# Second attention of a two-layer gated block on the context's own 64 columns, with tiles paired on halves of TensorE's array

## The chip, the cores and the metric

One core of one Trainium2 chip. The metric is the time of the whole kernel on the device in microseconds; lower is better. All operands are float32 unless a tile is declared BF16. The matrix engine is TensorE (PE), the others are VectorE (DVE), ScalarE (ACT), GpSimd (POOL) and SyncE (SP), which issues most DMAs.

## The reference

x has 4 batches of 256 rows of 128 (1,024 rows, 8 tiles of 128 rows); the context ctx_512 has 4 batches of 512 rows of 64. LN is a layer norm without weights.

```python
x = x + tanh(g_xattn[0]) * attention16(LN(x), ctx_512)       # self and cross attention, 16 heads of 8
x = x + tanh(g_ffn[0])   * routed_experts(LN(x))             # 8 experts, top 2, capacity 160 each pass
# second attention: one head of 128, over the context alone
q = LN(x) @ Wq + bq                  # Wq 128x128
k = ctx_512 @ Wk + bk                # Wk 64x128
v = ctx_512 @ Wv + bv                # Wv 64x128
x = x + tanh(g_xattn[1]) * softmax(q @ k.T) @ v
# dense experts: all 8 are computed for every row, 2 of them get a weight
x = x + tanh(g_ffn[1]) * sum_e c_e * (silu(h @ w1g_e.T) * (h @ w1u_e.T)) @ w2_e.T,  h = LN(x)
```

## The kernel before, in words

**The first layer** (lines 830 to 1461) is the attention with 16 heads and the routed experts. Here it matters in three places. At the start GpSimd makes constants (lines 679 to 726), the last two being the ones of the value tiles, and then helps to split queries and keys (`qk_r`, line 743). Then TensorE turns the 24 blocks of expert weights (`turn_weights`, line 1819) while ScalarE copies them out of PSUM (`take_weights`), and GpSimd puts the rows at their experts' slots (line 797); SyncE reads them back as `xs` (lines 644 and 646). `routed_experts` starts with `transpose_rows(0)`, which waits for those rows.

**Between the weights and the routed experts** stands `context(j)` on TensorE (line 1994): four products of 65x512 give the second attention's keys for the whole context (`k1_t`), sixteen of 65x128 give its values (`v1`). Row 64 of `c_t`, the turned context, holds ones for the bias. ScalarE copies the results out (lines 1039 to 1046). The first expert's products wait for these copies (`kv1_act`).

**The second attention** (TensorE from line 2064, ScalarE from 1081, VectorE from 1490) takes the rows that the routed experts have written back, in three groups, `BACK = ((0, 2), (2, 4), (4, 8))` tiles. `turn_back` turns the normalised rows, `queries1` multiplies them by Wq. Then per tile t, with two tiles (`QT`) to a batch: `scores1` (one product, 128x512), VectorE's `max1`, ScalarE's `exp1`, four turnings of the probabilities on TensorE (line 2091), ScalarE's `take_turned1`, `values1` (four products of 128x128), VectorE's `add_values` and row statistics. The order written out is: scores of t + 1, turning of t, values of t - 1. `unread(n)` are bf16 products of 512 columns that nobody reads.

**The dense experts** (`dense_experts`, lines 1935, 1375 and 1019) need the normalised rows of four tiles (`normalise(3, s)`), turned (`transpose_half(3, s)`) and copied (`take_ht`). Per unit i, that is a half s and an expert e: a pair of products of 128x512 on TensorE (line 1957), Silu on ScalarE, a product with `hidden` on VectorE (line 1399), four products down (line 1945), and `take_down` on VectorE. Units 0 to 14 follow each other in order; behind the pair of unit 1 `go_down(0)`, `transpose_half(3, 1)`, the pair of unit 2 and the router.

Semaphores that count: `p_in`/`p1_in` probabilities, `q1_act` queries copied, `x3_in` rows of the second attention finished, `hh_in` hidden products.

## Time and profile before

| | |
|---|---|
| median of 3 runs | 333.73 us (333.17 to 334.24) |
| profiled execution, span | 337.6 us; the page gives no other time of its own |
| TensorE busy | 312.9 us, 93% |
| VectorE busy | 220.8 us, 65% |
| ScalarE busy | 194.1 us, 57% |
| GpSimd busy | 115.7 us, 34% |
| mean granted clock of TensorE | 0.995 of full speed |

The span is from the first to the last instruction of one profiled execution, from which all starts and durations below come. A line number of a row is that of the kernel file. A float32 product appears as two matmul records, a float32 turning (transpose) as one. Records of products overlap in time since they are pipelined; in the chain of waits each piece has only the time that it adds.

### The profile page before, as it was taken

Reading aid. Unit: us, or ns where it says so; the run is one execution under the profiler, and the core shown is the slowest. Engines: PE = TensorE matmul, PEld = TensorE weight load, DVE = VectorE, ACT = ScalarE, POOL = GpSimd, SP = SyncE. Lnnn points to the kernel's source line nnn. Section 1 sums busy time; section 2 is a strip of 40 time slices with the busy share of each in tenths; the row PEclk is TensorE's granted clock in tenths of the full one; section 3 lists DMA queues with packets and bytes.
Section 4 is the critical chain, followed back from the end, with each engine's and each line's share of the span. In section 5 each row is a group of like instructions: output and inputs, shape, how many; then the busy total and the mean of one; then the engine's idle time right before and its main releaser. Section 6 shows DMA issues by size and latency. Waiting matters only on the chain.

```text
span 337.6 us, 7474 instructions
## 1 busy us (share of the span) xinstructions
PE 312.9 (93%) x2891; PEld 189.6 (56%) x2891; DVE 220.8 (65%) x532; ACT 194.1 (57%) x410; POOL 115.7 (34%) x200
## 2 busy tenths in 40 slices
PE   8998969989999999899977999999996899999995
PEld 3545733334443434344666677777794357776665
DVE  4998798888989889676242052333321956779665
ACT  3468588978888889787266733323336265512221
POOL 6476732327334333231775003444442211110000
PEclk9999999999999999999997999999999999999999
DMA  7855995940437006240441580000002200000101
GB/s 174 199 110 160 175 213 132 209 90 10 153 110 209 5 5 188 70 124 2 109 157 35 133 212 10 21 18 19 22 12 70 71 0 2 1 2 0 31 3 31
DMA packets 35827, 27.83 MB, mean 82 GB/s; under 512 B 5627, under 2 KB 33070, under 8 KB 35792
## 3 DMA queue, kind: packets, MB, share of 16 engines
q1 hardware_dynamic: 33965, 25.04, 29.7%
q0 software_dynamic: 1280, 1.88, 1.7%
q10 hardware_dynamic: 547, 0.44, 0.5%
q8 instruction: 23, 0.38, 0.5%
q14 instruction: 12, 0.10, 0.1%
HBM read 11.89 MB, written 5.26 MB: 51 GB/s over the span
## 4 chain that ended last, share of the span: by engine, by line
PE 73%; ACT 7%; DVE 6%; issue 5%; POOL 5%; DMA 2%; SPq 0%; DVEq 0%; POOLq 0%; ACTq 0%
PE psum L1682 11%; PE psum L1876 11%; PE psum L1957 8%; PE psum L1624 5%; PE psum L1648 5%; PE psum L1945 4%; PE psum L1864 4%; ACT qk_r L948 3%; PE psum L1814 2%; POOL rows_in L797 2%; PE psum L1651 2%; PE psum L2060 2%; PE psum L2052 1%; PE psum L1575 1%; PE psum L1869 1%
## 5 line engine op out<-in xcount | busy, mean ns | idle before, releaser
L1213 DVE TENSOR_REDUCE nmax<-psum 128x2 f32<-128x1024 f32 (+2 forms) x88 | 102.0, 1216 | 11.6 <-PE psum L1624 10.3
L948 ACT ACTIVATE parts<-psum 128x512 f32<-128x512 f32 (+1 forms) x88 | 45.2, 566 | 8.6 <-PE psum L1648 7.7
L1876 PE MATMUL psum<-p_more,kcat 128*128 128x320 f32 (+2 forms) x160 | 40.2, 396 | 0.9 <-DVE p_more L1346 0.7
L819 POOL DMA_INDIRECT rows_back<-qcat,back_at x24 | 22.9, 952 | 50.3 <-ACT qcat L981 43.1
L1876 PEld LDWEIGHTS psum<-p_more,kcat 128*128 128x128 f32 x160 | 26.1, 190 | 9.1 <-issue 0.9
L1350 DVE TENSOR_TENSOR qcat<-psum,qk_r 128x320 f32<-128x320 f32 (+2 forms) x40 | 16.6, 422 | 22.1 <-ACT qk_r L989 13.5
L989 ACT ACTIVATE qk_r<-psum 128x320 f32<-128x320 f32 (+2 forms) x40 | 15.2, 384 | 24.5 <-PE psum L1876 21.5
L1682 PE MATMUL psum<-parts,v_aug 128*18 128x256 f32 (+1 forms) x352 | 28.5, 369 | 0.0
L1957 PE MATMUL psum<-h_t,kcat 128*128 128x512 f32 x60 | 28.1, 594 | 0.0
L1682 PE MATMUL psum<-qk_r,v_aug 128*18 128x256 f32 (+1 forms) x160 | 27.4, 373 | 0.0
L1648 PE MATMUL psum<-qcat,kcat 64*128 64x256 bf16 x256 | 24.7, 271 | 1.9 <-ACT p_more L948 0.8
L1027 ACT ACTIVATE qk_r<-psum 128x512 f32<-128x512 f32 x15 | 9.0, 597 | 30.1 <-PE psum L1957 30.1
L1682 PE MATMUL psum<-qk,v_aug 128*18 128x256 f32 (+1 forms) x160 | 26.1, 363 | 0.0
L1624 PE MATMUL psum<-kcat,qcat 64*128 64x512 bf16 x128 | 24.9, 386 | 0.2 <-DMA qcat<-parts 0.2
L1346 DVE COPY p_more<-psum 128x320 f32<-128x320 f32 x8 | 3.9, 492 | 29.7 <-PE psum L1854 29.7
L948 ACT ACTIVATE qk_r<-psum 128x512 f32<-128x512 f32 (+1 forms) x40 | 21.0, 581 | 2.1 <-PE psum L1648 1.7
L948 ACT ACTIVATE qk<-psum 128x512 f32<-128x512 f32 (+1 forms) x40 | 20.0, 551 | 1.8 <-PE psum L1648 1.8
L971 ACT ACTIVATE kcat<-psum 128x512 f32<-128x512 f32 x24 | 12.9, 607 | 13.0 <-PE psum L1814 7.8
L1945 PEld LDWEIGHTS psum<-kcat,qcat 128*128 128x128 f32 x120 | 15.6, 191 | 6.3 <-issue 5.0
L1624 PEld LDWEIGHTS psum<-kcat,qcat 64*128 64x128 bf16 x128 | 6.1, 93 | 22.6 <-issue 11.9
L797 POOL DMA_INDIRECT rows_in<-h_rows,put_at x16 | 16.0, 1000 | 8.1 <-issue 5.2
L690 POOL TENSOR_SCALAR ln_rstd<-ln_mv 128x2 f32<-128x2 f32 (+2 forms) x10 | 2.6, 261 | 41.7 <-DVE ln_mv L1118 22.8
(249 smaller groups left out, 630.4 us busy)
## 6 DMA issues: line engine op xcount, KB each, us to landing
kcat<-parts SPq DMA_DIRECT2D x18, 192.0 KB, 3.8
qcat<-parts SPq DMA_DIRECT2D x21, 128.0 KB, 3.6
kcat<-ones_b SPq DMA_DIRECT2D x8, 192.0 KB, 4.6
kcat<-in_L_ffn_wi_gate_dram SPq DMA_DIRECT2D x6, 256.0 KB, 4.5
kcat<-in_L_ffn_wi_up_dram SPq DMA_DIRECT2D x6, 256.0 KB, 4.8
kcat<-in_L_ffn_wo_dram SPq DMA_DIRECT2D x6, 256.0 KB, 5.0
parts<-in_L_ffn_w_dram SPq DMA_DIRECT2D x3, 512.0 KB, 5.6
rows_in<-zeros SPq DMA_DIRECT2D x1, 1290.0 KB, 5.7
```

The lines of the kernel that those rows point to most:

```text
L797: pool.indirect_dma_start(out=rows_in[0:E * SLOTS, :], out_offset=bass.IndirectOffsetOnAxis(ap=put_at[:, k, t:t + 1], axis=0), in_=h_rows[ ...
L819: pool.indirect_dma_start(out=rows_back[:, :], out_offset=bass.IndirectOffsetOnAxis(ap=back_at[0:m, e, t:t + 1], axis=0), in_=eo[0:m, e % ...
L948: act.activation(p_slots[u % NPT][:, 0:w], s2_bank(s2_place[u])[:, 0:w], ACT.Exp, scale=SCALE).then_inc(p_in, 1)
L989: act.activation(sg[:, i % 2, 0:m], gate_up_bank(i, 0)[:, 0:m], ACT.Silu).then_inc(sg_in[0], 1)
L1213: dve.tensor_reduce(dst[:, :, n * g:n * (g + 1)], src.rearrange("p (r q k) -> p r q k", r=PAR, q=n), AX.X, ALU.max, negate=True).then_inc( ...
L1350: dve.tensor_tensor(hh[:, e % 2, f, first:end], gate_up_bank(i, 1)[:, 0:end - first], sg[:, i % 2, 0:end - first], ALU.mult).then_inc(hh_i ...
L1624: ins = pe.matmul(dst, q[:, S + t * P:S + (t + 1) * P], k[:, S:KW], start=True, stop=True)
L1648: ins = pe.matmul(dst[:, c * S:(c + 1) * S], k[:, key:key + P], q[:, S:QW], start=True, stop=True)
L1682: ins = pe.matmul(dst[:, cols], v_aug[:, at:at + 2 * HA], p, start=r == 0 and opens(n), stop=r == ROUNDS - 1, skip_group_check=True)
L1876: ins = pe.matmul(gate_up_bank(i, m)[:, 0:end - first], w_t[e][:, m, f * P:(f + 1) * P], xs_t[:, e % 2, first:end], start=True, stop=True)
L1945: ins = pe.matmul(bank(DN_BANK[n % 4])[:, t * P:(t + 1) * P], hh1[:, n % 2, t * P:(t + 1) * P], w1_t[:, e, 2, :], start=True, stop=True)
L1957: ins = pe.matmul(bank(2 + 2 * (i % 2) + m), w1_t[:, e, m, :], h_t[:, s * BANK:(s + 1) * BANK], start=True, stop=True)
```

## The change

The second attention no longer makes keys and values. With M = Wq Wk^T (128x64), the scores of a row h are (h M + bq Wk^T) times the context's own row, plus a number per row, h (Wq bk) + bq bk. So:

- `fold_weights1` on TensorE, in the place of `context`: turns `w1_q` and `w1_k`, and multiplies them into `mk` (M, the bias column, the offset column), with 3 unread products inside and 16 behind it. ScalarE makes `bq_wide` and two copies.
- `queries1` multiplies by M (64 columns out); a batch's two tiles go to PSUM rows 0 to 63 and 64 to 127. `offsets1` makes the number per row. `scores1(b)` does both tiles of a batch, each on 64 rows of the array, against `c_t`, whose rows 64 to 127 are now a second copy of the context.
- `max1` has a second instruction, which takes the offset off the maximum by a subtraction and adds it again (`s1_bias`).
- `sums1(b)` multiplies the turned probabilities by the context's rows (64 columns out, two tiles on the halves of the columns), VectorE copies the sums (`take_sums1`), and `values1(b)` multiplies both tiles at once by Wv, laid out twice in the block diagonal `w1_v2`. The value bias times the gate is added to x beforehand (`add_value_bias`).
- The order on all three engines is written out tile by tile. The first dense pair, `gate_up1(0)`, stands between `sums1(3)` and `values1(3)`; the wait for `x3_in` goes from unit 1 to unit 2.
- SyncE loads the context's rows again (`ctx_rows`) and copies `c_t` to its other half behind the dense experts' weights. GpSimd clears `w1_v2` at the start, and multiplies `b1v` by the gate ahead of the masks.
- Dense halves are turned into banks 2 and 1, not 0 and 1.

The diff, cut to its core:

```diff
+            sp.dma_start(ctx_rows, c_in).then_inc(ctx_again, 16)
+            sp.dma_start(c_t[DC:2 * DC, :], c_t[0:DC, :]).then_inc(ctx_again, 16)
...
+            pool.memset(w1_v2[:, :], 0.0).then_inc(w1v_zero, 1)
...
+                link(pool.tensor_scalar(b1v[:, :], b1v[:, :], tanh_g[:, 1:2], None, ALU.mult))
...
+            act.wait_ge(gw_in, 1)
+            act.activation(bq_wide, zeros[:, 0:D], ACT.Identity, bias=b1_col[:, :]).then_inc(bq_in, 1)
+            act.wait_ge(mk_full, 1)
+            act.activation(w1_turned, bank(TURN1_BANK)[:, 0:D + DC + 1], ACT.Copy).then_inc(mk_act, 1)
+            act.wait_ge(mk_full, 2)
+            act.activation(mk, bank(MK_BANK)[:, 0:MK_OFF + 1], ACT.Copy).then_inc(mk_act, 1)
...
+            take_offsets(0)
+            take_queries(1)
+            take_offsets(1)
             exp1(0)
-            take_queries(1)
-            for t in range(NT):
-                if t + 1 < NT:
-                    exp1(t + 1)
+            exp1(1)
+            take_turned1(0)
+            take_rows(2)
+            take_turned1(1)
+            exp1(2)
+            take_queries(2)
+            exp1(3)
+            take_offsets(2)
+            take_turned1(2)
+            take_turned1(3)
+            for t in range(4, NT):
+                exp1(t)
+            for t in range(4, NT):
                 take_turned1(t)
...
+                link(dve.tensor_reduce(s1_nmax[:, t:t + 1], s1_bank(t), AX.X, ALU.max, negate=True))
+                if t in (0, BACK[1][0], BACK[2][0]):
+                    dve.wait_ge(off1_in, [first for first, _ in BACK].index(t) + 1)
+                dve.scalar_tensor_tensor(out=s1_bias[:, t:t + 1], in0=s1_nmax[:, t:t + 1], scalar=s1_off[:, t:t + 1],
+                                         in1=s1_off[:, t:t + 1], op0=ALU.subtract, op1=ALU.add).then_inc(nm1_in, 1)
...
+            statistics(2, 2, x_sb)
             max1(0)
-            statistics(2, 2, x_sb)
-            for t in range(NT):
-                if t + 1 < NT:
-                    max1(t + 1)
-                reciprocal1(t)
-                if t == 0:
-                    normalise(2, 2, x_sb)
-                if t >= 1:
-                    add_values(t - 1)
-                if t == NT - 2:
-                    normalise(3, 0, x1_sb)
-            add_values(NT - 1)
+            max1(1)
+            normalise(2, 2, x_sb)
+            max1(2)
+            max1(3)
+            add_value_bias(0, TPH)
+            reciprocal1(0)
+            max1(4)
+            take_sums1(0)
+            max1(5)
+            add_values(0)
+            reciprocal1(1)
+            take_sums1(1)
+            max1(6)
+            max1(7)
+            add_values(1)
+            add_value_bias(TPH, NT)
+            reciprocal1(2)
+            take_sums1(2)
+            normalise(3, 0, x1_sb)
+            add_values(2)
+            reciprocal1(3)
+            take_sums1(3)
+            add_values(3)
...
+            def fold_weights1():
+
+                dst = bank(TURN1_BANK)
+                pe.transpose(dst[:, 0:D], w1_q[:, :], ident[:, :])
+                pe.transpose(dst[:, D:D + DC + 1], w1_k[:, :], ident[0:DC + 1, 0:DC + 1]).then_inc(mk_full, 1)
+                unread(N_UNREAD_FOLD)
+                pe.wait_ge(mk_act, 1)
+                pe.wait_ge(bq_in, 1)
+                pe.wait_ge(wt_in[0], W_LAST[MK_BANK] + 1)
+                wq, wk, dst = w1_turned[:, 0:D], w1_turned[:, D:D + DC + 1], bank(MK_BANK)
+                pe.matmul(dst[:, 0:DC + 1], wq, wk, start=True, stop=True)
+                for t in range(QT):
+                    pe.matmul(dst[t * DC:(t + 1) * DC, MK_BIAS:MK_BIAS + 1], wk[:, 0:DC], b1_col[:, :], start=True, stop=True)
+                pe.matmul(dst[:, MK_OFF:MK_OFF + 1], bq_wide, wk[:, DC:DC + 1], start=True, stop=True).then_inc(mk_full, 1)
+
+            fold_weights1()
+            unread(N_UNREAD_ROWS)
...
+                for t in range(first, end):
+                    dst = bank(Q1_BANK)[t % QT * DC:(t % QT + 1) * DC, (t - first) // QT * P:((t - first) // QT + 1) * P]
+                    ins = pe.matmul(dst, mk[:, 0:DC], h_t[:, t * P:(t + 1) * P], start=True, stop=True)
+                ins.then_inc(q1_full, 1)
...
+            def scores1(b):
+                pe.wait_ge(q1_act, next(s + 1 for s, (first, end) in enumerate(BACK) if QT * b < end))
+                if b == 0:
+                    pe.wait_ge(ctx_again, 32)
+                    pe.wait_ge(wt_in[1], E)
+                if b >= 2:
+                    pe.wait_ge(p1_in, QT * (b - 1))
+                for t in range(QT * b, QT * b + QT):
+                    half = slice(t % QT * DC, (t % QT + 1) * DC)
+                    pe.matmul(s1_bank(t), q1_t[half, b, :], c_t[half, b * SC:(b + 1) * SC],
+                              start=True, stop=True).then_inc(sc1_full, 1)
+
+            def turn1(t):
                 b = t // QT
-                pe.matmul(bank(t % 2), q1_of(t, t + 1), k1_t[:, b * SC:(b + 1) * SC],
-                          start=True, stop=True).then_inc(sc1_full, 1)
-
-            def values1(t):
-                pe.wait_ge(p1t_in, t + 1)
-                if t >= 2:
-                    pe.wait_ge(x3_in, t - 1)
+                pe.wait_ge(p1_in, t + 1)
+                if b >= 1:
+                    pe.wait_ge(p1t_in, t - QT + 1)
+                else:
+                    pe.wait_ge(off1_in, 2)
                 for c in range(CT):
-                    ins = pe.matmul(bank(4 + t % 2)[:, 0:D], p1_t[:, t % 2, c * P:(c + 1) * P], v1[:, CT * (t // QT) + c, :],
-                                    start=(c == 0), stop=(c == CT - 1))
-                ins.then_inc(o1_full, 1)
+                    ins = pe.transpose(bank(t % QT)[:, c * P:(c + 1) * P], p1[:, b % 2, t % QT, c * P:(c + 1) * P],
+                                       ident[:, :])
+                ins.then_inc(p1t_full, 1)
+
+            def sums1(b):
+                pe.wait_ge(p1t_in, QT * b + QT)
+                if b == 0:
+                    pe.wait_ge(q1_act, len(BACK))
+                else:
+                    pe.wait_ge(u1_in, b)
+                for c in range(CT):
+                    for t in range(QT):
+                        ins = pe.matmul(bank(U1_BANK)[t * DC:(t + 1) * DC, 0:P], ctx_rows[:, CT * b + c, :],
+                                        p1_t[:, b % 2, t, c * P:(c + 1) * P], start=(c == 0), stop=(c == CT - 1),
+                                        skip_group_check=True)
+                ins.then_inc(u1_full, 1)
+
+            def values1(b):
+                pe.wait_ge(u1_in, b + 1)
+                if b == 0:
+                    pe.wait_ge(off1_in, len(BACK))
+                else:
+                    pe.wait_ge(x3_in, QT * b)
+                pe.matmul(bank(O1_BANK)[:, 0:QT * D], u1_t[:, b % 2, :], w1_v2[:, :], start=True, stop=True).then_inc(o1_full, 1)
...
-            unread(2)
+            unread(1)
             scores1(0)
             turn_back(1)
+            offsets1(0)
+            unread(1)
+            queries1(1)
+            unread(2)
             scores1(1)
-            queries1(1)
-            for t in range(NT):
-                if 0 < t < NT - 1:
-                    scores1(t + 1)
-                pe.wait_ge(p1_in, t + 1)
-                if t >= 2:
-                    pe.wait_ge(p1t_in, t - 1)
-                elif t == 0:
-                    pe.wait_ge(wt_in[1], E)
-                for c in range(CT):
-                    ins = pe.transpose(bank(2 + t % 2)[:, c * P:(c + 1) * P], p1[:, t % 2, c * P:(c + 1) * P], ident[:, :])
-                ins.then_inc(p1t_full, 1)
-                if t == QUERIES_AT:
-                    queries1(2)
-                if t >= 1:
-                    values1(t - 1)
-                if t == ROWS_AT:
-                    turn_back(2)
+            offsets1(1)
+            unread(1)
+            turn1(0)
+            turn1(1)
+            turn_back(2)
+            queries1(2)
+            offsets1(2)
+            turn1(2)
+            scores1(2)
+            turn1(3)
+            sums1(0)
+            scores1(3)
+            values1(0)
+            sums1(1)
+            turn1(4)
+            values1(1)
+            turn1(5)
+            turn1(6)
+            sums1(2)
+            turn1(7)
+            values1(2)
             transpose_half(3, 0)
-            values1(NT - 1)
+            sums1(3)
+            gate_up1(0)
+            values1(3)
             dense_experts()
```

## Rows read from the trace of the kernel before

**Rows 1.** windows: us, busy us of each engine (instructions), PEclk, DMA share, GB/s

```profile
184.50:191.50 7.00, 7.00 (x42) 5.08 (x41) 0.00 (x0) 5.00 (x9) 0.00 (x0) 1.00 0.41 107
265.00:275.70 10.70, 9.60 (x44) 5.33 (x44) 8.68 (x34) 5.44 (x13) 2.38 (x4) 1.00 0.00 0
275.70:289.90 14.20, 13.93 (x91) 10.96 (x92) 8.74 (x37) 8.31 (x19) 1.27 (x2) 1.00 0.01 2
```

**Rows 2.** chain of waits, start-up and before the routed experts: start, us added, what

```profile
21.64 1.65 POOL qk_r L743
...
180.05 4.50 PE psum L1814 x24
184.55 3.44 PE psum L2002 x8
187.99 3.57 PE psum L2006 x32
```

**Rows 3.** chain of waits, second attention and first dense units

```profile
265.26 0.50 PE psum L2036 x2
265.75 0.43 PE psum L2028 x2
...
280.11 0.86 PE psum L2052 x2
280.97 0.44 PE psum L2091 x4
281.41 0.89 PE psum L2060 x8
...
289.92 3.49 PE psum L1957 x8
...
294.74 1.72 PE psum L1957 x4
296.46 1.68 PE psum L1842 x16
```

**Rows 4.** timeline of ScalarE, two places: start, duration, instruction

```profile
185.23 0.60 ACT L971 ACTIVATE kcat<-psum 128x512 f32<-128x512 f32 x1 [0.39 <-PE psum L1814]
...
269.45 0.69 ACT L1072 ACTIVATE qk<-psum,s_nmax 128x512 f32<-128x512 f32 x1 [0.20 <-DVE s_nmax L1466]
```

**Rows 5.** groups by line from 190 us: busy us, mean ns | idle before

```profile
L1399 DVE TENSOR_TENSOR qcat<-psum,qk_r 128x512 f32<-128x512 f32 x15 | 10.4, 690 | 9.5 <-ACT qk_r L1027 9.5
...
L1027 ACT ACTIVATE qk_r<-psum 128x512 f32<-128x512 f32 x15 | 9.0, 597 | 30.1 <-PE psum L1957 30.1
...
L1466 DVE TENSOR_REDUCE s_nmax<-psum 128x1 f32<-128x512 f32 x8 | 5.5, 682 | 2.3 <-PE psum L2052 2.3
...
L1478 DVE SCALAR_TENSOR_TENSOR x_sb<-psum,s_rec,x_sb 128x128 f32<-128x128 f32 x8 | 2.8, 351 | 4.2 <-PE psum L2060 3.7 <-DVE s_rec L1488 0.4
...
L1470 DVE BATCH_NORM_STATS2 ln_stats<-x_sb 128x6 f32<-128x128 f32 x8 | 2.1, 282 | 0.0
...
L1488 DVE TENSOR_TENSOR s_rec<-s_rec,tanh_g 128x1 f32<-128x1 f32 x8 | 1.3, 160 | 0.3
```

**Rows 6.** line 646, the second load of each expert's rows, SyncE

```profile
L646 SPq DMA_DIRECT2D parts<-rows_in x8: 451/451/525, 186.0 to 194.0; - x8
...
DMA to landing us min/median/max: 2.0/2.3/2.3
```

**Rows 7.** timeline of GpSimd at start-up

```profile
21.00 0.55 POOL L726 MEMSET v_aug<- 128x256 f32 x1
```

**Rows 8.** timeline of TensorE in pass 1, bf16 scores on row halves

```profile
102.28 0.39 PE L1624 MATMUL psum<-kcat,qcat 64*128 64x512 bf16 x2
```

**Rows 9.** chain of waits, routed experts' products on column halves

```profile
201.83 0.61 PE psum L1869 x16
```

**Rows 10.** windows around the low granted clock, columns as in rows 1

```profile
179.00:180.00 1.00, 0.00 (x0) 0.00 (x0) 0.20 (x2) 0.69 (x2) 0.49 (x1) 1.00 0.18 58
...
181.00:182.00 1.00, 1.00 (x7) 0.97 (x6) 0.69 (x3) 1.00 (x3) 0.76 (x1) 0.50 0.14 43
```

199 lines of the change are left out of this document (106 added, 93 removed).

## The prediction

> **What bounds the kernel now.** I read the windows by stretch first, then the chain of waits, then the groups by line. The windows [rows 1] show TensorE busy for all of 184.5 to 191.5, for 9.6 of 10.7 us up to 275.7 and for 13.93 of 14.20 us up to 289.9, while VectorE has 8.74 and ScalarE 8.31 us of work in the last stretch: TensorE sets the pace there, the others have room. The chain [rows 2] gives the first stretch to the context projections, 3.44 + 3.57 = 7.0 us. It gives the second attention a period of 0.86 (scores) + 0.44 (turning) + 0.89 (values) = 2.19 us per tile [rows 3], then the dense products, which run without a gap from 289.92 to the end. So the end moves by whatever moves (a) the first routed expert and (b) the point from which dense products are gapless, the third pair at 294.74 [rows 3].
>
> **Part 1, the projections become a folded weight.** Removed: 7.0 us of TensorE. Added: two turnings (0.2), three unread products (0.215 each by the pair that takes 0.43 [rows 3]: 0.65), a wait for ScalarE, four small products, sixteen unread products (3.45). ScalarE ends its last weight copy near 185.8 [rows 4], then widens the bias and copies 193 columns, together at most what 512 columns cost, 0.59 [rows 5], which lets TensorE go on near 186.5. The four small products are bound by weight loads; the router's eight products with 8 columns take 1.68, 0.21 each [rows 3], two of ours have half the columns: 0.7. Then 187.2 + 3.45 = 190.7, against 191.5 where the projections end (184.55 + 7.0). Rows cannot be turned much earlier anyway: the first two loads issue by 186.0 and land 2.3 us later, near 188.5 [rows 6]. Gain 0.7; I take **-0.6**, bounds -1.2 (all small products hidden) and 0. The expert loop behind is TensorE's own work and keeps the gain. Two new transfers of 0.5 MB each are queued on SyncE behind the expert weights; behind them there only stands the read back, which waits for the last expert anyway: 0.
>
> **Part 2, start-up.** GpSimd clears w1_v2 (128x256) ahead of the value ones; the same size takes 0.55 [rows 7], and the chain runs through GpSimd right behind it, at 21.64 [rows 2]. Bounds 0 and +0.55; the chain behind is largely TensorE, so I take **+0.4**. The product for b1v on GpSimd stands ahead of masks, and TensorE's values wait for masks; today's block of three there delays nobody, so 0, its own length if that cover is gone. One more small load on SyncE, and its wait for the clearing some 30 us old: 0.
>
> **Part 3, the second attention.** TensorE's work from the first turned row to the third dense pair, before: turned rows 16 x 0.11, unread 4 x 0.215, queries 1.72 (1,024 columns, two times the 0.86 of 512), scores 8 x 0.86, turning 8 x 0.44, values 8 x 0.89, two dense pairs 3.44 (3.49 in the chain), one down product group, four of 128 columns like the values, 0.89: 26.2 us, from 265.26 to 294.74 [rows 3], so 3.3 idle. After:
> - Scores of two tiles on row halves. The bf16 scores of pass 1 do this: two of 512 columns take 0.39 together, so they start together [rows 8]. So a pair 0.91, 4 x 0.91 = 3.64, for 6.88; bound 1.72 a pair if the halves don't run together.
> - Queries on column halves, 8 products of 128 columns. The routed down products on halves take 0.61 for 8 of 64 columns [rows 9]; one after another 8 x 0.111 = 0.89, fully paired 0.44. I take 0.17 each (0.11 to 0.22): 1.4.
> - Sums: 32 products of 128 columns on column halves; serial 1.78 a batch, paired 0.89. I take 1.0 a batch. Values: 4 of 256 columns, 0.43 each.
> - Offsets, 8 with one column, weight-bound: 0.21 each, 1.7. Three more unread: 0.65.
>
> New work: 23.5 us, 2.7 less. That gain needs VectorE and ScalarE to keep pace, and this is where I expect it to fail. VectorE's work per tile: maximum 0.69, value add 0.35, row statistics 0.28, two small ones 0.16 [rows 5], 1.64. New are per tile a bias instruction that waits for the maximum (0.17 and a gap of 0.04), per batch a copy of the sums (128 columns; between 0.16 for one and 0.69 for 512 that is 0.29), and twice an addition over 512 columns (0.69 [rows 5]), less four pairs of small instructions: 8 x 0.21 + 4 x 0.29 + 1.4 - 4 x 0.39 = +2.7. And each wait in VectorE's order holds what is behind it.
>
> I laid the four queues out, each instruction at the later of its engine being free and its semaphore, with durations as above, 0.75 for an exponential and its read of the sum (the first alone 0.69 [rows 4]) and 0.59 for ScalarE's copies of 512 columns. For the kernel before this gives 290.05 for the first dense pair and 294.82 for the third (trace: 289.92 and 294.74 [rows 3]). For the new one:
> - statistics of the last four tiles stand ahead of the first maximum, and the first exponential also waits for offsets 1: it starts at 271.9, not 269.45 [rows 4].
> - queries 2 need rows 2 and tiles 0, 1 turned: the third batch's scores start at 277.3; VectorE sits idle 3.2 us before maximum 4.
> - maximum 5 stands behind the sums copy, maxima 6 and 7 behind add_values(0), reciprocals and sums copy 1: exponentials 6 and 7 end at 285.7. ScalarE turns tile 4 only behind them, though it was ready at 282.6. TensorE idles 2.3 us before turning tile 6.
> - sums 2 end near 288, normalise(3,0) stands behind their copy; first dense pair 290.8. It holds values(3) for 1.72: VectorE idles 1.8, and hidden(0) starts at 294.8, statistics, GpSimd and normalise(3,1) behind it: third pair **297.5**.
>
> So idle grows from 3.3 to 8.7, +5.4 for -2.7 of work: +2.7 against the layout of the kernel before. Bounds: +1.7 with queries, sums, gaps at their low ends, +5.6 with the column halves serial. From the third pair on the queues are as before. The early product itself is worth nothing here: what follows waits for VectorE.
>
> A rule against the sum: today the change from whole-array products to column halves and back shows 0.61 where full pairing is 0.44, so entry and exit cost at most 0.09 each [rows 9]. The new order has 21 such changes. I put them in TensorE's idle time, 0; all on the path they are 1.9, and the sum below would be +4.4. The Trainium skill (TensorEngine Tiling (Array Packing), Key Properties) says that a change of tiling mode drains TensorE; the trace agrees only as far as those 0.09 us leave room for a short drain.
>
> **Sum.** -0.6 + 0.4 + 2.7 = +2.5. The profiled span is 337.6, the median of the three runs 333.73; the page gives no other time of that execution. I add the difference to the median: **336.2 us**. A measurement can tell about 0.3% (1.0 us) from no change.
>
> **Rivals.**
> 1. *TensorE still sets the pace.* VectorE and ScalarE run ahead enough for idle time to stay at 3.3; then the 2.7 us of work come off: -2.7 - 0.6 + 0.4 = -2.9, **330.8**. For it: 14.20 us hold 8.74 of VectorE [rows 1]. Against: the waits in its queue. It decides if maxima 4 to 7 follow each other without waits, that is if tile 4 is turned before 284. Chance 0.17; a halfway case within 1.0 of no change 0.10.
> 2. *The clock falls.* TensorE was idle about 2 us from 178.1 and the granted clock went from 1.00 to 0.50 (2.4 to 1.2 GHz) from 181 [rows 10]; 24 turnings took 4.50 [rows 2] for 24 x 0.11 = 2.64. My layout has idle times of 2.3 us at 284 and about 1 us near 186. A fall costs 4.50 - 2.64, about 1.9: **338.1**. Chance 0.15.
> 3. *Row halves run one after another in f32*, so scores don't do what the change says: +3.2 more, **339.4**. Chance 0.05; no f32 product on row halves is in the trace, bf16 ones are.
> 4. *The tiling changes cost 0.09 each on the path*: 336.2 + 1.9 = **338.1**, chance 0.04. The drain that the Trainium skill (same page and section) names would be this case.
> The rest, 0.49, is the forecast, 334.7 to 337.8.
>
> **Numbers.** The likeliest case is 336.2. Slower by over 0.3%: 0.49 + 0.15 + 0.05 + 0.04 = 0.73; within 0.10; faster 0.17. The range goes from 332.0, leaving out most of rival 1, to 338.8, leaving out rival 3 and the high bound of the halves.
>
> **What would show it.** The first routed turning 0.6 earlier; the experts' cadence unchanged; the first exponential 2.5 us later relative to the first turned row; two scores in 0.9 together; VectorE idle some 3 us before maximum 4, TensorE some 2 us before turning tile 6; the third dense pair 2.7 us later against the first turned row; granted clock 1.00 throughout. I am wrong if TensorE's idle time there stays under 5 us, if the sums take 1.8 a batch, or if the early part shifts by over 1 us.

## The result, and the profile after

| | before | after |
|---|---|---|
| median | 333.57 us (333.17 to 334.24, 4 runs) | 336.62 us (336.10 to 339.91, 4 runs) |
| ratio after to before | | 1.0104, 95% interval 1.0066 to 1.0142 |
| profiled execution, span | 337.6 us | 334.7 us, its own time 336.49 us |
| mean granted clock | 0.995 | 0.999 |

The change costs 1.04%, 3.05 us; the forecast was 336.2. A time is its span plus 1.7 to 1.8 us in every execution that gives both, so the profiled execution of before, with its span of 337.6, must have taken about 339.4 us, well over its median; adding a difference to the median, as the forecast did, allows for that. The spans of the two profiles must not be subtracted. The kernel before was therefore profiled again with the first experiments (`before_again`: span 333.5, time 335.32). Executions with a mean granted clock of 0.998 or more are called undisturbed below; in the profiled ones of the others the clock stood at or near 0.50 for 2 us or more, and the others are mostly 1 to 3 us longer.

**The second attention.** The chain of waits of the kernel after, from the first turned row to the third dense pair, answers to [rows 3]:

```profile
259.32 0.49 PE psum L2103 x2
259.82 0.43 PE psum L2066 x2
...
264.18 1.06 PE psum L2134 x4
265.24 0.55 PE psum L2121 x4
266.08 0.68 ACT qk L1104 x2
266.80 0.66 PE psum L2145 x4
...
269.91 0.98 PE psum L2121 x8
270.89 0.50 PE psum L2145 x4
271.39 1.06 PE psum L2134 x4
...
277.44 0.61 DVE s_nmax L1507
...
279.96 0.50 ACT qcat L1112
...
280.59 0.63 PE psum L2145 x4
281.22 1.02 PE psum L2157 x16
...
285.09 1.91 PE psum L2006 x4
287.00 0.45 PE psum L2168 x2
287.44 0.02 issue
287.47 0.61 DVE x_sb L1532 x2
...
289.28 1.04 POOL ln_rstd L714
...
290.75 1.10 PE psum L1902 x4
291.84 1.72 PE psum L2006 x4
```

L2103 turns the rows, L2134 makes the scores of a pair of tiles, L2121 the offsets, L2145 turns the probabilities, L2157 makes the sums, L2168 the values, L2006 is a dense pair. The stretch takes 291.84 - 259.32 = 32.52 us. Before it took 29.48 [rows 3], and 29.49 in `before_again` (261.15 to 290.64). That is +3.04. In all three profiles the end comes 42.86 us after the third pair (334.7 - 291.84, 337.6 - 294.74, 333.5 - 290.64). The medians differ by 3.05 us. So, as near as the medians can tell, the whole difference lies in this stretch, and the change ahead of it is worth about nothing.

Windows over just this stretch, with the columns of [rows 1], first `before_again`:

```profile
261.15:290.64 29.49, 28.38 (x155) 19.15 (x156) 20.66 (x81) 16.23 (x35) 4.72 (x7) 1.00 0.00 1
```

then the kernel after:

```profile
259.32:291.84 32.52, 28.31 (x192) 17.00 (x193) 23.10 (x87) 16.41 (x38) 5.06 (x7) 1.00 0.00 1
```

TensorE is busy as long as before, 28.3 us, though its products should need 2.7 us less; VectorE has 2.4 us more; TensorE's idle time grows from 1.1 to 4.2 us. The timelines of VectorE and of ScalarE show where it waits:

```profile
272.54 0.69 DVE L1507 TENSOR_REDUCE s_nmax<-psum 128x1 f32<-128x512 f32 x1 [3.57 <-PE psum L2134]
...
265.81 0.26 ACT L1096 ACTIVATE s_off<-psum,qcat 128x2 f32<-128x2 f32 x1 [1.76 <-PE psum L2121]
265.98 0.68 ACT L1104 ACTIVATE qk<-psum,s_bias 128x512 f32<-128x512 f32 x1
...
278.33 0.69 ACT L1104 ACTIVATE qk<-psum,s_bias 128x512 f32<-128x512 f32 x1 [2.27 <-DVE s_bias L1510]
```

VectorE stands 3.57 us before maximum 4. ScalarE stands 2.27 us before exponential 6, because maxima 6 and 7 are in VectorE's line behind the values of batch 0 (277.44 in the chain). TensorE in turn stands 1.96 us before it turns tile 6, at 280.59. This is one chain: a wait in one engine's fixed order is passed on to the next.

**Ahead of the experts.** The chain of the kernel after no longer runs through products there; it answers to [rows 2]:

```profile
180.36 0.97 POOL rows_in L822
181.33 0.30 issue
181.63 2.22 DMA rows_in<-h_rows,put_at
...
184.26 2.21 DMA parts<-rows_in
186.51 0.66 PE psum L1920 x3
...
187.90 3.47 PE psum L1942 x12
```

GpSimd sends the rows to the experts in 16 puts from 161.08 on. The last put's own transfer takes 2.22 us, a load brings the rows back in 2.21 us, and TensorE, done with the sixteen unread products, waits 0.53 us for them (L1920 is the first routed turning).

### The profile page after: what moved, and what is told of

Read it like the earlier page. It is cut to its first block, busy times and chain, and to the rows that moved or that the text cites. A ratio compares the mean times of both kernels' runs of the same rounds, so it can differ in the third digit from the quotient of the medians.

```text
span 334.7 us, 7533 instructions
## 1 busy us (share of the span) xinstructions
PE 309.5 (92%) x2917; PEld 183.5 (55%) x2917; DVE 223.7 (67%) x538; ACT 190.3 (57%) x408; POOL 116.7 (35%) x202
## 4 chain that ended last, share of the span: by engine, by line
PE 68%; ACT 8%; POOL 7%; DVE 6%; DMA 5%; issue 5%; SPq 1%; DVEq 0%; ACTq 0%; POOLq 0%
PE psum L1748 11%; PE psum L1942 11%; PE psum L2006 7%; PE psum L1690 5%; PE psum L1714 5%; POOL rows_in L822 4%; PE psum L2020 4%; PE psum L1930 4%; ACT qk_r L973 3%; PE psum L1717 2%; PE psum L1641 1%; PE psum L2134 1%; PE psum L1935 1%; ACT parts L973 1%; DMA x_sb<-in_x_dram 1%
## 5 line engine op out<-in xcount | busy, mean ns | idle before, releaser
L2006 PE MATMUL psum<-h_t,kcat 128*128 128x512 f32 x60 | 28.3, 594 | 0.0
L713 POOL TENSOR_SCALAR ln_rstd<-ln_mv 128x2 f32<-128x2 f32 (+2 forms) x10 | 2.7, 273 | 44.2 <-DVE ln_mv L1523 22.3
```

Of the source, the lines that this page charges most:

```text
L2006: ins = pe.matmul(bank(2 + 2 * (i % 2) + m), w1_t[:, e, m, :], h_t[:, s * BANK:(s + 1) * BANK], start=True, stop=True)
```

## The experiments

The median of the undisturbed executions of the kernel before, taken anew beside each of three groups of experiments, is 333.6, 333.5 and 333.8 us (13 of 25, 14 of 22 and 5 of 13 executions); for the kernel after it is 336.5 (three of four). Four of those 32 took 334.8 to 335.2 us at a full clock too, so a median of three is rough.

**before_again**: the kernel before, unchanged.

> The kernel before, unchanged, for a second profile. The first one's span of 337.6 us lies 3.9 above the median time, while the changed kernel's span of 334.7 lies 1.8 below the time of the same execution (336.49). Theory A: the first profile was taken from an execution disturbed between 169 and 191 us, where the granted clock fell to 0.50; this one has a span of 331.5 to 332.5, the first product of the routed experts near 187.9, and the projections end within 0.5 us of the moment at which the first rows land, so the folded weight is worth under 0.3 us. From the first turned row to the third dense pair 29.5 us, as in the first profile. Theory B: the first profile was typical and only its overhead differs; then the span is 337 again and the first product stands at 192.7. The time itself is the same in both: 333.2 to 334.0.

334.35 us (10 runs), ratio 0.9999 (0.9970 to 1.0028). The stretch takes 29.49 us, so [rows 3] were sound. The span of 333.5 lies between the two theories: the first profile was not typical, so theory B falls, but theory A's undisturbed start of the experts was not met either (first expert product at 189.76, not 187.9). Here too the clock fell before the experts, as windows of this execution show:

```profile
174.00:176.00 2.00, 2.00 (x13) 1.96 (x13) 1.47 (x12) 1.19 (x2) 1.39 (x3) 0.60 0.13 37
176.00:178.00 2.00, 2.00 (x19) 1.98 (x17) 1.12 (x7) 1.20 (x3) 1.70 (x2) 0.55 0.19 57
```

**no_unread_rows**: the sixteen unread products ahead of the routed experts left out.

```diff
-        N_UNREAD_FOLD, N_UNREAD_ROWS = 3, 16
+        N_UNREAD_FOLD, N_UNREAD_ROWS = 3, 0
```

> The changed kernel without the 16 unread products behind the folded weight. Theory A (the first rows' landing at 186.5 sets the start of the routed experts, the products only fill the wait): the first turned row stays at 186.5, same time within 0.5 us, unless the granted clock falls in the 4 us of idle time that this leaves, which would cost 1.5 to 3 us and show as 0.50 in the windows near 187 to 190. Theory B (TensorE's own queue sets it): 0.5 to 3 us faster.

341.21 us, ratio 1.0175 (1.0127 to 1.0224), 4.6 us over the kernel after. The first routed turning comes 25.39 us after GpSimd's first put (163.22 to 188.61), for 25.43 in the kernel after: the rows' landing sets it, as theory A has it. The first twelve expert products take 6.29 us, for 3.47 in the kernel after. Windows ahead of and under them, with the clock at 0.50:

```profile
186.00:188.00 2.00, 0.00 (x0) 0.00 (x0) 0.00 (x0) 0.20 (x1) 0.00 (x0) 0.50 0.29 77
188.00:190.00 2.00, 0.99 (x3) 0.47 (x3) 0.29 (x1) 0.00 (x0) 0.00 (x0) 0.50 0.56 147
190.00:192.00 2.00, 1.65 (x3) 1.18 (x4) 0.20 (x1) 0.00 (x0) 0.00 (x0) 0.50 0.59 151
```

Not all of the 4.6 us belongs to the edit: in the profiled execution the first put itself came 2.1 us later (163.22 for 161.08), ahead of the place of the edit. From the first put to the end it takes 3.3 us more than the kernel after (340.1 - 163.22 against 334.7 - 161.08), and the shortest of the four, 339.84, lies 3.3 above the undisturbed median. So the products that nothing reads are part of the change: without them it would cost some 3.3 us more, a little over the 1.5 to 3 that theory A gave.

**unread_rows_24**: 24 of them instead (same line, 24 for 16).

> The changed kernel with 24 products that nothing reads ahead of the routed experts instead of 16, so TensorE has 8 times 0.225 us = 1.8 us more to do there, which is part of what the change took away. If the rows' landing (GpSimd's index work and two transfers) sets the start of the experts, with the 0.53 us that TensorE waits for it: the first routed turning moves by 1.3 us, the time by 1.3 us to 337.9. If TensorE set it, 1.8 us, 338.4. If something later absorbs it: 336.6.

First put to first routed turning: 162.46 to 189.13 = 26.67 us, against 161.08 to 186.51 = 25.43 in the kernel after: +1.24, as the landing of the rows predicts (1.8 less the wait of 0.53). TensorE has half a microsecond of room there, no more. The time, 339.82 us, is 3.2 over the kernel after and not 1.3: none of its four executions was undisturbed. In the profiled one the first put already came 1.4 us later (162.46 for 161.08), and the clock also fell in the second attention (0.50 at 274 to 276).

**memset_late**: GpSimd's clearing of w1_v2 behind the fillings with ones.

```diff
             const(pool.memset(e_base[:, :], math.e))
-            pool.memset(w1_v2[:, :], 0.0).then_inc(w1v_zero, 1)
             const(pool.memset(v_of(0, NT, HD, HA), 1.0))
             const(pool.memset(v_of(NT, NT + NC, HD, HA), 1.0))
+            pool.memset(w1_v2[:, :], 0.0).then_inc(w1v_zero, 1)
```

> The changed kernel with GpSimd's clearing of the doubled value weight behind its two fillings with ones instead of ahead of them. The 0.4 us that the prediction put on this start-up step stays in GpSimd's line, so if GpSimd's first product of the splitting waits for all of them, nothing moves: GpSimd's qk_r instruction at 21.75 us and the first put of rows at 161.08 as in the changed kernel, time 336.6 us. If a wait for the ones on another engine carries the step: 0.1 to 0.4 us earlier, time 336.2 to 336.5 us.

339.25 us, four disturbed executions, which says nothing on the edit. GpSimd's own timeline does. From GpSimd's L690 (14.46) to qk_r (21.64) the kernel before needs 7.18 us. The same way (L713 to L767) is 14.32 to 21.75 = 7.43 after the change, and 14.46 to 21.88 = 7.42 here. So the clearing takes 0.25 us of GpSimd's line wherever it stands, 0.31 long and partly overlapped, not the 0.55 of a filling of the same size [rows 7]. Further on it can't be found: the first put of rows stands at 160.91 in `before`, and at 161.08, 160.81 and 160.52 in the kernel after, gate_behind and bias_dropped. The timeline of GpSimd in the kernel after, where L748 is the clearing:

```profile
20.50 0.31 POOL L748 MEMSET w_v<- 128x256 f32 x1
20.74 0.32 POOL L749 MEMSET v_aug<- 128x128 f32 x1
21.12 0.54 POOL L750 MEMSET v_aug<- 128x256 f32 x1
21.75 1.64 POOL L767 TENSOR_TENSOR qk_r<-qk,parts 128x768 f32<-128x768 f32 x1
```

**gate_behind**: the last values ahead of the early dense product.

```diff
             sums1(3)
-            gate_up1(0)
             values1(3)
+            gate_up1(0)
```

> The changed kernel with values(3) ahead of the first dense pair. Theory A (VectorE's queue sets the pace, and the early pair holds values(3) for 1.7 us): first dense pair 1.2 us later, hidden(0) 0.3 earlier, third pair and end 0.8 us earlier, 335.8. Theory B (TensorE sets the pace, so that filling its wait with the pair is a gain, as the change intends): 0.5 to 1.5 us slower.

The stretch takes 259.29 to 290.96 = 31.67 us, 0.85 less; undisturbed executions 335.7 (median of four), 0.8 less; all ten 337.1, ratio 1.0057 (1.0030 to 1.0085). The early product is not merely worth nothing, it costs 0.85: behind it values(3) waited, and behind those the statistics, GpSimd's root and the next turning.

**act_order**: ScalarE copies turned tiles 4 and 5 ahead of exponentials 6 and 7.

```diff
-            for t in range(4, NT):
-                exp1(t)
-            for t in range(4, NT):
-                take_turned1(t)
+            for t in (4, 6):
+                exp1(t)
+                exp1(t + 1)
+                take_turned1(t)
+                take_turned1(t + 1)
```

> The changed kernel with ScalarE copying the turned tiles 4 and 5 ahead of exponentials 6 and 7. Theory A (the copies of tiles 4 and 5 stand behind exponentials that VectorE delays): TensorE's idle time of 2 us before it turns tile 6 falls below 1.2, third pair and end 0.5 us earlier, 336.1. Theory B (ScalarE's order is as good as any, since TensorE or VectorE alone sets the pace): within 0.2 us of the changed kernel.

A miss for theory A; the time is within the 0.2 us of theory B. All ten: 337.5 us, ratio 1.0092 (1.0060 to 1.0123); three undisturbed ones have a median of 336.35 against 336.5, so nothing was gained that the runs can tell, where 0.4 to 0.5 was expected. The profiled execution had a fall of the clock (0.50 at 272 to 274), so its stretch (33.83 us) can't be compared. Its timeline hints at why: exponential 6 no longer waits for its maximum but stands behind the copy of tile 5, which waits 0.68 us for its turning, and TensorE still stands 1.35 us before it turns tile 6 (1.96 in the kernel after, under 1.2 expected). One hold gave way to another; in an undisturbed execution that is not shown.

**no_offset** and **bias_dropped**. The first leaves the offsets out: products, ScalarE's readings, and VectorE's join to the maximum. The exponential gets the negated maximum alone; a shift of a whole row leaves a softmax as it is.

```diff
-            take_offsets(0)
...
-            offsets1(0)
...
-                link(dve.tensor_reduce(s1_nmax[:, t:t + 1], s1_bank(t), AX.X, ALU.max, negate=True))
-                if t in (0, BACK[1][0], BACK[2][0]):
-                    dve.wait_ge(off1_in, [first for first, _ in BACK].index(t) + 1)
-                dve.scalar_tensor_tensor(out=s1_bias[:, t:t + 1], in0=s1_nmax[:, t:t + 1], scalar=s1_off[:, t:t + 1],
-                                         in1=s1_off[:, t:t + 1], op0=ALU.subtract, op1=ALU.add).then_inc(nm1_in, 1)
+                dve.tensor_reduce(s1_nmax[:, t:t + 1], s1_bank(t), AX.X, ALU.max, negate=True).then_inc(nm1_in, 1)
```

> The changed kernel without the offset of each row (the product of the turned row with the folded key bias, its reading by ScalarE, and VectorE's instruction that joins it to the maximum); the exponential takes the negated maximum alone. The shift of a row drops out of a softmax, so only the rounding differs. My theory, that the second attention is paced by a ring of ScalarE and VectorE with TensorE waiting in it: the stretch from the first turned row to the third dense pair, 32.52 us in the changed kernel, loses the three offset readings that stand ahead of exponentials and the eight joins of 0.22 us: 30.4 to 30.7 us, time 334.6 us. The rival, that VectorE's joins alone cost it: the same 2.0, but then the kernel that keeps products and readings and drops only the joins gains all of it too. A second rival, that only the last batch counts (maxima 6 and 7 behind the values of batch 0): 32.52 less 0.5.

The second has the last part of that edit alone.

> The changed kernel with the offsets' products and ScalarE's readings of them kept, unused: VectorE's join of 0.22 us after each maximum and its wait for the offset go, and the exponential takes the negated maximum alone. My theory (ScalarE's readings and the waits for them are most of what the offsets cost): the stretch of 32.52 us falls by 0.4 to 0.8, the time to 336.0 us. The rival (VectorE's joins are the cost): it falls by 2.0, to 30.5, the time to 334.6 us. If TensorE's own work set the pace, it would not change at all.

no_offset: stretch 260.99 to 291.04 = 30.05 us (-2.47); undisturbed 334.0 (five), all ten 334.93, ratio 1.0038 (1.0000 to 1.0076). bias_dropped: 258.77 to 290.85 = 32.08 us (-0.44); undisturbed 336.1 (three), all seven 337.07, ratio 1.0098 (1.0066 to 1.0130). VectorE's joins are 8 x 0.22 us of work and cost 0.44; products and readings cost the other 2.0. That goes against both rivals: the joins alone would have taken the 2.0 with them, the last batch alone 0.5. How the 2.0 divide is not shown. The readings stand in line ahead of exponentials, as the theory has it; exp_first below puts one of them at about 0.6. But the products are TensorE's work too: it is busy 26.31 us in the stretch of no_offset against 28.07 in bias_dropped, 1.76 less, and no run keeps the products without their readings.

**exp_first**: exponential 0 ahead of ScalarE's reading of the second group's offsets.

```diff
-            take_offsets(1)
             exp1(0)
+            take_offsets(1)
```

> The changed kernel with exponential 0 ahead of ScalarE's reading of the second group's offsets, for which it stands 1.76 us idle with exponential 0 behind it in line. My theory (the late first exponential is carried to the end, since the turning of its tile stands ahead of the last group's queries and of the third batch's scores): exponential 0 starts 1.6 us earlier, the stretch of 32.52 us falls by 0.7, the time to 335.9 us. The rival (what comes later binds alone, as with the copies ahead of exponentials 6 and 7): exponential 0 earlier by as much and the stretch unchanged, 336.6 us.

Exponential 0 starts 5.03 us after the first turned row, for 6.66 in the kernel after, 1.6 earlier as expected. From the first turned row (259.03) the first turning of probabilities (265.93) comes 6.90 us later, in the kernel after 7.48; the third batch's scores 11.40 for 12.07; the turning of tile 6 20.60 for 21.27. So the late first exponential is carried through, 0.6 to 0.7 of it. It is not more because the first turning has a wait of its own for the same reading (`off1_in`), and stands 0.44 us for it. Then the clock fell in this profiled execution, the sums of the third batch took 1.91 for 1.02, and the stretch came to 33.19. One execution of four was undisturbed, 335.87 us, 0.6 under the kernel after; with one, that is a hint, not a proof. All four: 337.34, ratio 1.0100 (1.0046 to 1.0154).

**unread_4**: four unread products, not one, ahead of the first turning of probabilities.

```diff
             offsets1(1)
-            unread(1)
+            unread(4)
             turn1(0)
```

> The changed kernel with four products that nothing reads instead of one ahead of the turning of tile 0, where TensorE waits 0.79 us for exponential 0: 3 more of 0.22 us, all inside that wait. Theory A, that the executions at a lower mean clock (0.995 and under, some 1 to 3 us longer; in one profiled kernel of this family the clock stood at 0.50 around 272 us) come from TensorE's pauses between 266 and 271 us, the first of which this fills: more of the executions have a mean clock of 0.998 or more, the median is 336.2 us, the stretch of 32.52 us unchanged. Theory B, that the clock falls for pauses elsewhere (start-up, the landing of the rows): the same mixture and median as before, 336.6 to 337. If the products reach past the wait: 0.1 to 0.3 us longer.

337.92 us (four, none undisturbed), ratio 1.0138 (1.0085 to 1.0191). The added products fit: the turning of tile 6 comes 21.28 us after the first turned row, as in the kernel after (21.27). But the clock fell at the next pause, TensorE's 2.0 us before tile 6, in windows:

```profile
278.00:280.00 2.00, 0.48 (x5) 0.24 (x3) 1.93 (x8) 1.74 (x5) 0.00 (x0) 1.00 0.00 0
280.00:282.00 2.00, 1.55 (x10) 1.25 (x12) 1.30 (x7) 1.33 (x3) 1.50 (x2) 0.65 0.00 0
282.00:284.00 2.00, 2.00 (x18) 1.67 (x15) 0.56 (x3) 0.05 (x1) 0.12 (x1) 0.50 0.00 0
```

Theory A is not borne out: filling the first pause kept the clock in none of the four. In this execution the clock fell right behind another pause of the stretch. The stretch took 259.17 to 292.93 = 33.76, 1.24 more. Windows of memset_late show it fall earlier, behind a window in which TensorE was idle 0.69 us:

```profile
270.00:272.00 2.00, 1.31 (x16) 1.00 (x14) 0.48 (x3) 1.82 (x5) 0.00 (x0) 1.00 0.00 0
272.00:274.00 2.00, 2.00 (x13) 1.11 (x12) 0.00 (x0) 1.61 (x5) 0.00 (x0) 0.77 0.00 0
274.00:276.00 2.00, 2.00 (x8) 0.89 (x8) 0.91 (x2) 0.07 (x1) 0.00 (x0) 0.50 0.03 8
```

**retimed**: no_offset in another order, as the lists of calls in full, with t for the turning of a tile and its copy, e exponentials, m maxima, r reciprocals, u sums, v and a values, q queries, s scores, R rows, b turned rows, x unread, h and g the first dense turning and pair, n22 and n30 the normalised rows, vb the value bias, st statistics:

```diff
-TensorE: b0 x2 q0 x1 s0 b1 x1 q1 x2 s1 x1 t0 t1 b2 q2 t2 s2 t3 u0 s3 v0 u1 t4 v1 t5 t6 u2 t7 v2 h0 u3 g0 v3
+TensorE: b0 x2 q0 x1 b1 s0 x1 q1 x2 s1 x1 t0 b2 t1 q2 t2 s2 u0 t3 s3 v0 u1 t4 t5 v1 t6 u2 t7 u3 v2 h0 v3 g0
-ScalarE: R0 q0 R1 q1 e0 e1 t0 R2 t1 e2 q2 e3 t2 t3 e4 e5 e6 e7 t4 t5 t6 t7
+ScalarE: R0 q0 R1 q1 e0 e1 t0 R2 e2 q2 t1 e3 t2 e4 t3 e5 e6 t4 t5 e7 t6 t7
-VectorE: st m0 m1 n22 m2 m3 vb r0 m4 u0 m5 a0 r1 u1 m6 m7 a1 vb r2 u2 n30 a2 r3 u3 a3
+VectorE: st m0 m1 n22 m2 m3 r0 vb m4 r1 m5 u0 m6 a0 u1 m7 a1 u2 r2 vb n30 u3 a2 r3 a3
```

> The kernel without offsets, in another order on three engines: the early dense product behind the last values, ScalarE copies turned tiles of a batch before the exponentials of the batch after the next, maxima 4 to 7 each ahead of the values of the batch two before, the sums of the last batch ahead of the values of the third. Nothing else differs. My theory (work is enough narrower; it is the order on ScalarE and VectorE that lost it): the stretch from the first turned row to the third dense pair takes 26.1 to 27.0 us against 32.52 in the changed kernel and 29.48 in the one before, TensorE idle in it under 4 us, and the time is 330.5 to 331.5 us, faster than the kernel before by 0.7 to 0.9%. The rival (a step that no order takes away, such as the longer way from a turned row to its exponential and pair-wise sums, sets 29 us or more): 29 to 30 us, time 333.5 us.

330.97 us (330.49 to 333.38, ten), ratio 0.9913 (0.9878 to 0.9948): faster than both kernels, 0.9% faster than the one before. The stretch takes 261.97 to 288.74 = 26.77 us, in one window:

```profile
261.97:288.74 26.77, 25.43 (x176) 15.19 (x177) 21.99 (x79) 15.86 (x35) 4.71 (x7) 1.00 0.00 1
```

TensorE idles 1.3 us. VectorE does 22.0 us of work in 26.8, more than in the kernel before (20.7 in 29.5), and holds none of exponentials 4 to 7 for more than 0.52 us (2.27 in the kernel after).

**retimed_offsets**: all instructions of the kernel after, reordered in a similar way (the two new orders are not the same).

```diff
-TensorE: b0 x2 q0 x1 s0 b1 o0 x1 q1 x2 s1 o1 x1 t0 t1 b2 q2 o2 t2 s2 t3 u0 s3 v0 u1 t4 v1 t5 t6 u2 t7 v2 h0 u3 g0 v3
+TensorE: b0 x2 q0 x1 s0 b1 o0 x1 q1 x2 s1 o1 x1 t0 b2 q2 t1 o2 s2 u0 t2 s3 t3 v0 t4 u1 t5 v1 t6 u2 t7 u3 v2 h0 v3 g0
-ScalarE: R0 q0 R1 o0 q1 o1 e0 e1 t0 R2 t1 e2 q2 e3 o2 t2 t3 e4 e5 e6 e7 t4 t5 t6 t7
+ScalarE: R0 q0 R1 o0 q1 o1 e0 e1 t0 R2 q2 t1 e2 o2 e3 e4 t2 t3 e5 e6 t4 t5 e7 t6 t7
-VectorE: st m0 m1 n22 m2 m3 vb r0 m4 u0 m5 a0 r1 u1 m6 m7 a1 vb r2 u2 n30 a2 r3 u3 a3
+VectorE: st m0 m1 n22 m2 vb m3 r0 m4 r1 u0 m5 m6 a0 u1 m7 a1 vb u2 r2 n30 u3 a2 r3 a3
```

> The changed kernel with its offsets and all its instructions, in another order: the early dense product behind the last values; exponentials 4 and 5 ahead of the copies of turned tiles 2 and 3, copies 4 and 5 ahead of exponential 7; maxima 5 and 6 ahead of the values of batch 0 and 7 ahead of those of batch 1; the turning of tile 1 behind the queries of the last group; sums of the last batch ahead of the values of the third. My theory (order on ScalarE and VectorE cost about 3 us and the offsets about 2.5, two separate terms): the stretch from the first turned row to the third dense pair takes 28.2 to 29.0 us against 32.52 in the changed kernel, the time is 332.3 to 333.2 us, just under the kernel before. The rival (the order is only worth its 3 us once the offsets are gone, since ScalarE's readings of them hold the exponentials): 30.5 us or more, time 334.5 us.

The stretch takes 261.44 to 290.85 = 29.41 us, 0.4 outside the theory's range and nearer to it than to the rival: order alone gives back 3.1 us. The three undisturbed executions are at 333.6, level with the kernel before (332.3 to 333.2 was expected); all ten 335.61, ratio 1.0036 (0.9994 to 1.0078). The same stretch in one window:

```profile
261.44:290.85 29.41, 26.33 (x191) 16.97 (x193) 23.44 (x87) 16.40 (x38) 5.06 (x7) 1.00 0.01 1
```

So the terms are nearly separate: order 3.1 (32.52 to 29.41) and 3.3 (30.05 to 26.77), offsets 2.5 and 2.6.

## Why the prediction was right, and where its steps were not

The stretches account for the undisturbed times:

| kernel | stretch, us | less 29.48 | undisturbed median less 333.6 |
|---|---|---|---|
| after | 32.52 | +3.0 | +2.9 |
| gate_behind | 31.67 | +2.2 | +2.1 |
| bias_dropped | 32.08 | +2.6 | +2.5 |
| no_offset | 30.05 | +0.6 | +0.4 |
| retimed_offsets | 29.41 | -0.1 | 0.0 |
| retimed | 26.77 | -2.7 | -2.8 |

**Part 3, forecast +2.7, measured +3.04.** The marks of the layout were met step by step. Counted from the first turned row: first exponential at 6.66 us (259.32 to 265.98), 2.46 later than before (4.20: 261.15 to 265.35 in `before_again`), forecast 2.5; scores of the third batch at 12.07, forecast 12.04; VectorE idle 3.57 before maximum 4, forecast 3.2; TensorE idle 1.96 before tile 6, forecast 2.3; first dense pair at 25.8, forecast 25.5; third pair at 32.5, forecast 32.2. That waits from the written order make the difference is shown by retimed_offsets: the same instructions in another order take 3.1 us less, as much as the change had cost. Leaving out the offsets in the old order takes off 2.5.

**The step that failed inside it** is the balance "New work: 23.5 us, 2.7 less" with "idle grows from 3.3 to 8.7". The windows show no less busy time (28.38 before, 28.31 after) and idle time up by 3.1 to 4.2, not by 5.4 to 8.7. By the prediction's own sign, "I am wrong if TensorE's idle time there stays under 5 us", this step was wrong.

Three things stand between the forecast work of 23.5 us and the 28.3 that the window counts as busy. The first is counting: the window counts 28.4 us as busy in the kernel before too, where the chain's prices make 26.2, so 2.2 us of the difference were there already. The second goes with the order. Retimed_offsets has the same instructions and the same 21 changes between whole-array and half-array products, and its window counts 26.33 us as busy, 2.0 less than the kernel after. Of these 2.0, 0.87 come with the early product (27.44 busy in gate_behind): with it the turning of the dense rows (L1902) takes 1.10 us, tile by tile behind VectorE's `h_rows`, and 0.44 without. So part of what the window calls busy is waiting, which the layout had counted as idle. The third is work that the forecast left out: 0.7 us by the window of retimed_offsets (26.33 - 23.5 - 2.18), 1.4 by that of retimed (25.43 - 21.8 - 2.18, with the offsets at their forecast 1.7). Both are estimates.

So in the layout's own counting the work fell by 1.3 to 2.0 us, not 2.7, and the idle time came to some 8 us, not 8.7. The term that was mis-sized is "I put them in TensorE's idle time, 0" for the changes between whole-array and half-array products, and the two small errors partly cancel, which is luck; the sign of 5 us was set in a measure that the profile does not use. Chain of waits of retimed, where TensorE hardly waits:

```profile
273.20 0.59 PE psum L2140 x4
273.79 1.06 PE psum L2131 x4
274.85 0.63 PE psum L2161 x2
275.47 1.02 PE psum L2152 x16
276.50 1.02 PE psum L2140 x8
277.52 0.43 PE psum L2161 x2
```

and of before_again:

```profile
280.39 0.86 PE psum L2052 x2
281.25 0.44 PE psum L2091 x4
```

L2152 makes the sums, L2140 and L2091 turn probabilities, L2131 and L2052 make scores, L2161 values. Turning one tile takes 0.44 us behind a whole-array score or another turning, and 0.59 behind sums on column halves. Two in a row take 1.02, so only the first pays. Values take 0.43 behind a turning and 0.63 behind scores on row halves. So a whole-array product right behind one on halves takes 0.15 to 0.2 us longer. What going the other way costs is not separated: a pair of scores takes 1.06 against 0.86 for one tile before, which holds both the entry and the pairing. The prediction took 0.09 from [rows 9] as the most that an entry or an exit could be. Ten such exits at 0.15 to 0.2 would be 1.5 to 2 us, an estimate above the 0.7 to 1.4 of the windows, so not every exit costs that much. The Trainium skill (TensorEngine Tiling (Array Packing), Key Properties) says that a change of tiling mode drains TensorE; by these rows the trace agrees, at 0.15 to 0.2 us for the first product back on the whole array. Rival 4 named a cost that is real and priced it too low; how much of it reached the time of the kernel after no run separates.

**Part 1, forecast -0.6, measured near 0.** The step that failed is "190.7, against 191.5 where the projections end": the 191.5 was read from a profile in which the clock had fallen shortly before ([rows 10]; 24 turnings in 4.50 us), and the 190.7 follows from it. Its bound for the rows, "near 188.5", comes from the same profile, in which the last put came 22.4 us after the first (160.91 to 183.34); in `before_again` and in the kernel after it comes 20.6 us after it. What starts the experts after the change is the rows' landing, 25.43 us after GpSimd's first put; TensorE had been done since 185.98, 0.53 us early, not at 190.7. The prediction had that bound ("Rows cannot be turned much earlier anyway") and still booked a gain. By the undisturbed medians less part 3, parts 1 and 2 together are 2.9 - 3.0, about -0.1, which is within what such medians can tell. In `before_again` the projections ended late and the first expert product came 1.2 us later after the first put than in the kernel after (189.76 - 161.77 = 27.99 against 26.82): in a disturbed execution of the kernel before the shorter work does pay. There TensorE worked without a pause through 4 us at mean clocks of 0.60 and 0.55, which cost it about 1.7 us by these figures; without that its projections would have ended 25.1 us after the first put, just ahead of the rows. That is an estimate: no undisturbed execution of the kernel before was profiled.

**Part 2, forecast +0.4, measured +0.25 in GpSimd's line** and nothing that can be told from the first put on: within its bounds 0 and 0.55, mis-sized by taking a filling with ones for a clearing.

**"The early product itself is worth nothing"** was wrong by its sign: gate_behind puts it at 0.85 us of cost. The prediction's own line named the reason ("It holds values(3) for 1.72").

**Rival 1** (TensorE sets the pace, 330.8) fell for this kernel. Its number comes back, at 330.97, for the reordered one without offsets, but that is a coincidence: rival 1 kept the offsets, whose work the forecast had at 1.7 us, and booked 0.6 for part 1. Its condition, maxima 4 to 7 without waits between them, retimed nearly brings about (one wait of 0.65 us, before maximum 6). **Rival 2** (the clock falls, 338.1) is not the median but is real: it shows in the profiled executions of act_order, unread_rows_24, memset_late, exp_first and unread_4, at 270 to 278 or at 278 to 284, and costs the stretch 1.2 to 1.6 us there, not the 1.9 of the forecast. One of the four executions of the kernel after took 339.91 at a mean clock of 0.990. **Rival 3** fell: four records of scores on row halves take 1.06 us, 0.2 more than the two of one tile.

## What to carry to other kernels

When work is made narrower in a kernel with fixed orders, lay out each engine's queue again: here the order cost 3.1 us and the offsets 2.5, while the kernel without both is 2.8 us faster than the one before. A wait is paid by whatever stands behind it in line: move small results that nobody needs yet (offsets, copies, an early product) behind the work that the next engine waits for. Compare two profiles by stretches between marks of the same execution, and only where neither lost the clock. Set a sign of being wrong in the measure in which it will be read: the layout's idle time of 8.7 us is not the idle time of a window, which came to 4.2.

## What the runs showed of the hardware

- A whole-array f32 product right behind products on halves takes longer: a turning 0.59 us behind products on column halves for 0.44, values 0.63 behind products on row halves for 0.43, also where nothing is waited for. The same kernel has a turning of 0.54 behind values, which is no change of tiling, so 0.10 of such a difference can have another cause.
- f32 products on two row halves do run together: two tiles' scores of 512 columns in 1.06 us, where two on the whole array take 2 x 0.86.
- GpSimd clears 128x256 f32 in one piece in 0.31 us; the filling of as many elements in a slice of v_aug takes 0.54, 0.55 in [rows 7].
- TensorE's clock goes from 1.00 to 0.50 (2.4 to 1.2 GHz) behind pauses of 0.7 to 2 us in one execution and not in the next, with nearly the same instructions ahead: behind the pause before tile 6 it fell in unread_4 and exp_first and not in the kernel after. Undisturbed are 35 of 70 executions of the kernel before, and 22 of 67 of the kernel after and those of its variants that keep such pauses in the second attention (all but no_unread_rows and retimed); retimed, which hardly pauses there, has 6 of 10. But the kernel before alone ranges from 3 of 10 in before_again to 14 of 22, so whether such pauses make a fall likelier is not settled. What decides it in one execution stays open.
